# Joining two state scans into one instruction in a fused selective-scan and feed-forward kernel

## The reference

```python
dt  = softplus(dt_r @ dt_proj_w.T + dt_bias)          # per channel and token
A   = -exp(A_log)                                     # per channel and state
dA  = exp(dt_t[..., None] * A)                        # decay
dBx = dt_t[..., None] * B_t[:, None, :] * x_t[..., None]   # inflow
h   = dA * h + dBx                                    # state
y   = einsum('bdn,bn->bd', h, C_t)                    # sum over the states
```

## Time and profile before

| | us |
|---|---|
| median of three runs | 4897.68 |
| profiled execution, whole | 4888.99 |
| its span, first to last instruction | 4887.2 |
| dt*x of one step to the next, ordinary step | 34.42 to 34.43 |
| the same across the seventh step of a chunk | 37.04 |
| across the eighth | 38.95 |
| across the first of the next | 43.04 |

### The profile page before, as it was taken

One profiled execution on the slowest core, in us unless ns is written; L12 is line 12 of the kernel. 1 busy time (PEld: TensorE's weight loads), 2 busy tenths in 40 slices (PEclk: granted clock), 3 DMA queues, 4 the chain that ended last, 5 costly groups with the idle time before them and its releaser, 6 DMA issues.

```text
span 4887.2 us, 73028 instructions
## 1 busy us (share of the span) xinstructions
PE 4584.8 (94%) x22816; PEld 3921.1 (80%) x22816; DVE 4506.2 (92%) x7793; ACT 3554.9 (73%) x8720; POOL 3922.7 (80%) x2218
## 2 busy tenths in 40 slices
PE   7788989999999999999999999999999999999889
PEld 6667778888887888888888788888888888887668
DVE  3999989999999999999999999999999999999991
ACT  3677777777777777777777777777777777777660
POOL 0888878888787888888888887888888888888880
PEclk9889999999999999999999999999999999999999
DMA  7324243343434334343353434334343343434222
GB/s 252 118 76 157 101 150 131 114 175 123 167 134 148 139 130 167 123 167 122 123 181 117 171 127 159 131 122 171 133 168 120 131 162 123 162 120 146 87 107 93
DMA packets 157828, 677.85 MB, mean 139 GB/s; under 512 B 18816, under 2 KB 27648, under 8 KB 108288
## 3 DMA queue, kind: packets, MB, share of 16 engines
q1 hardware_dynamic: 139008, 639.62, 36.9%
q10 hardware_dynamic: 18432, 33.56, 1.8%
HBM read 618.06 MB, written 55.05 MB: 138 GB/s over the span
## 4 chain that ended last, share of the span: by engine, by line
POOL 61%; issue 20%; PE 8%; DVE 4%; DMA 3%; ACT 2%; POOLq 1%; SPq 1%; DVEq 0%; ACTq 0%
POOL dbx L444 38%; POOL half L452 19%; POOL dtx L467 3%; DVE hb L1289 2%; DMA bb<-bc_scratch 2%; PE g L695 2%; PE gx L525 2%; PE ys L505 1%; PE hb L788 1%; DMA ybuf<-in_wf_scales 1%; DMA bc_scratch<-ssmT 1%; DVE hc L1236 1%; ACT hb L997 1%; PE ys L545 1%; POOL x L460 1%
## 5 line engine op out<-in xcount | busy, mean ns | idle before, releaser
L1289 DVE TENSOR_TENSOR_SCAN hb<-hb,hstate,dbx 128x256 f32<-128x256 f32 x4096 | 2838.8, 738 | 140.0 <-ACT hb L997 86.8
L444 POOL TENSOR_TENSOR dbx<-dtx,bb 128x1024 f32<-128x1024 f32 x1024 | 2416.4, 2360 | 438.4 <-DVE hb L1289 347.3
L997 ACT ACTIVATE hb<-dt,a_neg 128x256 f32<-128x256 f32 x4096 | 1789.4, 468 | 66.6
L452 POOL TENSOR_TENSOR half<-hc 128x512 f32<-128x512 f32 x1024 | 1302.0, 1271 | 301.3 <-DVE hc L1236 270.5
L1236 DVE TENSOR_TENSOR hc<-hb,cb 128x512 f32<-128x512 f32 x2048 | 1373.0, 670 | 0.0
L505 PE MATMUL ys<-half,ident 128*128 128x256 f32 x4096 | 1109.3, 395 | 165.6 <-POOL half L452 165.5
L505 PEld LDWEIGHTS ys<-half,ident 128*128 128x128 f32 x4096 | 766.2, 195 | 327.4 <-POOL half L452 223.8
L545 PE MATMUL ys<-xnT,wz 128*128 128x256 f32 x4096 | 968.1, 391 | 57.8 <-DVE ybuf L1247 57.8
L695 PE MATMUL g<-ybuf,wo 128*128 128x256 f32 x3840 | 948.6, 391 | 0.7 <-issue 0.7
L545 PEld LDWEIGHTS ys<-xnT,wz 128*128 128x128 f32 x4096 | 784.9, 196 | 193.9 <-DVE ybuf L1247 89.2
L525 PE MATMUL gx<-xnT,wx 128*128 128x256 f32 x3968 | 900.5, 380 | 2.0 <-issue 1.6
(11 more groups left out here) (104 smaller groups left out, 2482.2 us busy)
## 6 DMA issues: line engine op xcount, KB each, us to landing
wz<-in_win SPq DMA_DIRECT2D x128, 1024.0 KB, 4.8
wx<-in_win SPq DMA_DIRECT2D x124, 1024.0 KB, 4.8
wo<-in_wout SPq DMA_DIRECT2D x123, 1024.0 KB, 5.0
wf<-wf_scratch SPq DMA_DIRECT2D x113, 512.0 KB, 3.3
xc_scratch<-xcn ACTq DMA_DIRECT2D x128, 256.0 KB, 2.0
xcs<-xc_scratch SPq DMA_DIRECT2D x128, 256.0 KB, 5.0
bb<-bc_scratch SPq DMA_DIRECT2D x64, 512.0 KB, 7.3
cb<-bc_scratch SPq DMA_DIRECT2D x64, 512.0 KB, 6.4
```

The lines of the kernel that those rows point to most:

```text
L444: nc.gpsimd.tensor_tensor(dbx[:, k % 2, :].rearrange("p (n t) -> p n t", n=NQ), dtx[:, a * T:(a + 1) * T].unsqueeze(1).to_broadcast([P, NQ ...
L452: nc.gpsimd.tensor_tensor(half[:, k % 4, :], hc[:, k % 2, 0:HALF], hc[:, k % 2, HALF:GW], ALU.add).then_inc(halves, 1)
L997: ins = nc.scalar.activation(h[:, m * T:(m + 1) * T], dt[:, j % 2, a * T:(a + 1) * T], ACT.Exp, scale=a_neg[:, ds((2 * j + a) * N + 2 * v ...
L1289: ins = nc.vector.tensor_tensor_scan(h[:, m * T:(m + 1) * T], h[:, m * T:(m + 1) * T], dbx[:, k % 2, (2 * w + m) * T:(2 * w + m + 1) * T], ...
```

## The change

The scan of a unit becomes one instruction of 128x512 over both states, with a constant 0.0 as its initial value. For that, column 0 of every decay is made zero, and column 0 of every inflow is made the whole state at the chunk's first token: the carried state times the first decay, plus the first inflow.

- Column 0 of `dt` holds a constant 1e19, so that exp(dt*A) is 0 there (`A` is held at or below -1e-16). Softplus writes columns 1 to 255 of both tiles in one instruction and the two first columns into `dt0`. The bias of dt moves into the matmul as a 65th row, so `ssmT` and `ssn` get one row more.
- ScalarE computes `decay0` (two instructions of 128x16) between softplus and the skip term.
- GpSimd gets `inflow_of` (dt*x of the first columns, then of the others), moved ahead of inflow 7 of the step before; `carry_of` (first inflows from a broadcast `b0`, and decay0*hstate); and `replace_first`, which writes column 0 of the B rows `bb`: once per tile of a pair, but for the first tile of a chunk once per group.
- For groups 1 and 5 of a step GpSimd adds the two remaining 256-column parts too, and TensorE sums them with one matmul in place of two.
- SyncE stores and loads the sixteen first values of B per chunk.

The core of the diff:

```diff
+FAR, LEAST_A = 1e19, 1e-16
@@ SyncE
             def bc_rows(chunk):
                 sp.wait_ge(ss_evac, after(chunk + 1))
-                sp.dma_start(bc_dram[chunk], ssmT[R:E, :]).then_inc(bc_st, 16)
-                sp.wait_ge(bc_st, landed(chunk + 1))
+                sp.dma_start(bc_dram[chunk], ssmT[BC:EO, :]).then_inc(bc_st, 16)
+                sp.dma_start(b0_dram[chunk].unsqueeze(1), ssmT[BC:BC + N, 0:1]).then_inc(bc_st, 16)
+                sp.wait_ge(bc_st, landed(2 * (chunk + 1)))
+                sp.dma_start(b0[:, chunk % 2, :], b0_dram[chunk].partition_broadcast(P)).then_inc(b0_in, 16)
@@ GpSimd
+            nc.gpsimd.memset(dt[:], FAR).then_inc(zeroed, 1)
+            def replace_first(a, lo, hi):
+                nc.gpsimd.tensor_tensor(bb[:, lo:hi, 0], carried[:, a * N + lo:a * N + hi], inflow0[:, a, lo:hi],
+                                        ALU.add).then_inc(b_first, 1)
             def group_of_b(S, k, chunk):
                 a, q = divmod(k, NQ)
+                fresh = S % PAIRS == 0 and a == 0
+                pool.wait_ge(bb_in[q], landed(chunk + 1))
+                if k == 0:
+                    pool.wait_ge(inflow, after(S + 1))
+                    pool.wait_ge(carry, after(S + 1))
+                if fresh:
+                    replace_first(a, NQ * q, NQ * (q + 1))
+                    pool.wait_ge(b_first, after(first_inflows(S) + q + 1))
+                elif q == 0:
+                    pool.wait_ge(dbxs, after(8 * S + k))
+                    replace_first(a, 0, N)
+                    pool.wait_ge(b_first, after(first_inflows(S) + (3 if S % PAIRS == 0 else 0) + a + 1))
                 pool.wait_ge(scans, after(UNITS * S + 2 * k - 2))
...
             def group_sum(S, k):
...
+                both = nc.gpsimd.tensor_tensor(half[:, k % 4, :], hc[:, k % 2, 0:HALF], hc[:, k % 2, HALF:GW],
+                                               ALU.add)
+                if k % NQ != 1:
+                    both.then_inc(halves, 1)
+                    return
+                both.then_inc(pair_sums, 1)
+                pool.wait_ge(pair_sums, after(2 * S + k // NQ + 1))
+                nc.gpsimd.tensor_tensor(half[:, k % 4, 0:T], half[:, k % 4, 0:T], half[:, k % 4, T:HALF],
                                         ALU.add).then_inc(halves, 1)
...
+            def inflow_of(S):
+                pool.wait_ge(sp_act, after(S + 1))
+                pool.wait_ge(xc_in[S % 2], landed(S // 2 + 1))
+                nc.gpsimd.tensor_tensor(dtx0[:], dt0[:, S % 2, :], xcs[:, S % 2, 0:2 * T:T], ALU.mult
+                                        ).then_inc(dtx0_ready, 1)
...
+            def carry_of(S):
...
+                nc.gpsimd.tensor_tensor(inflow0[:], dtx0[:].unsqueeze(2).to_broadcast([P, 2, N]),
+                                        b0[:, chunk % 2, :].unsqueeze(1).to_broadcast([P, 2, N]), ALU.mult
+                                        ).then_inc(inflow, 1)
+                pool.wait_ge(first_decays, after(S + 1))
+                pool.wait_ge(kept, after(UNITS * (S - PAIRS + 1)))
+                nc.gpsimd.tensor_tensor(carried[:], decay0[:], hstate[:, 2 * j * N:2 * (j + 1) * N], ALU.mult
+                                        ).then_inc(carry, 1)
@@ GpSimd, one step
                     for k in range(1, 8):
+                        if k == 7 and zz:
+                            inflow_of(S + 1)
                         group_of_b(S, k, c)
...
                     if zz:
-                        next_step(S + 1)
+                        carry_of(S + 1)
+                        group_of_b(S + 1, 0, (S + 1) // PAIRS)
                     group_sum(S, 6)
@@ TensorE, group_sum
-                for i in range(2):
+                for i in range(1 if q == 1 else 2):
@@ ScalarE, pair_softplus
-                for a in range(2):
-                    ins = nc.scalar.activation(dt[:, q % 2, a * T:(a + 1) * T], ys[1][:, a * T:(a + 1) * T],
-                                               ACT.Softplus, bias=dtb[:, ds(2 * jq + a, 1)])
-                ins.then_inc(sp_act, 1)
+                nc.scalar.activation(dt0[:, q % 2, :], ys[1][:, 0:2 * T:T], ACT.Softplus)
+                nc.scalar.activation(dt[:, q % 2, :, 1:T], ys[1][:].rearrange("p (a t) -> p a t", a=2)[:, :, 1:T],
+                                     ACT.Softplus).then_inc(sp_act, 1)
                 nc.scalar.preload_act_table_set(BASE)
+                act.wait_ge(sp_act, after(q + 1))
+                act.wait_ge(carry, after(q))
+                for a in range(2):
+                    ins = nc.scalar.activation(decay0[:, a * N:(a + 1) * N], a_neg[:, (2 * jq + a) * N:(2 * jq + a + 1) * N],
+                                               ACT.Exp, scale=dt0[:, q % 2, a:a + 1])
+                ins.then_inc(first_decays, 1)
@@ VectorE, scan
-                        for m in range(2):
-                            ins = nc.vector.tensor_tensor_scan(
-                                h[:, m * T:(m + 1) * T], h[:, m * T:(m + 1) * T],
-                                dbx[:, k % 2, (2 * w + m) * T:(2 * w + m + 1) * T],
-                                hstate[:, ds((2 * j + a) * N + 2 * v + m, 1)], ALU.mult, ALU.add)
-                        ins.then_inc(scans, 1)
+                        nc.vector.tensor_tensor_scan(h[:], h[:], dbx[:, k % 2, w * UW:(w + 1) * UW], 0.0, ALU.mult,
+                                                     ALU.add).then_inc(scans, 1)
```

More of the change, by code:

```diff
@@ L22 @@
 E = R + 2 * N
+EO = E + 1
+BC = R + 1
 NQ = 4
@@ L83, in build_program @@
 def build_program(nc, x, win, wout, wf_codes, wf_scales, ffn_bias, xproj, dtw_in, convw_in, convb_in,
-                  dtb_in, alog_in, dparam_in, lnw_in, out):
+                  alog_in, dparam_in, lnw_in, out):
     ctx = ExitStack()
@@ L144, in build_program @@
         ssm = sb("ssm", [P, TT, E])
-        ssn = sb("ssn", [P, TT, E])
+        ssn = sb("ssn", [P, TT, EO])
         sq = sb("sq", [P, TT, E])
         ssq = sb("ssq", [P, 6])
-        ssmT = sb("ssmT", [E, T])
-        dt = sb("dt", [P, 2, 2 * T])
-        dtx = sb("dtx", [P, 2 * T])
+        ssmT = sb("ssmT", [EO, T])
+        dt = sb("dt", [P, 2, 2, T])
+        dtx = sb("dtx", [P, 2, 2, T])
+        dt0 = sb("dt0", [P, 2, 2])
+        dtx0 = sb("dtx0", [P, 2])
+        b0 = sb("b0", [P, 2, N])
+        decay0 = sb("decay0", [P, 2 * N])
+        carried = sb("carried", [P, 2 * N])
+        inflow0 = sb("inflow0", [P, 2, N])
         gate = sb("gate", [P, 2, 2 * T])
@@ L837, in _ @@
             nc.scalar.preload_act_table_set(BASE)
-            act.wait_ge(zeroed, after(4))
+            act.wait_ge(zeroed, after(8))
             def norm_start(n, mv, rstd, nmr, stats, ln, r, nm):
@@ L929, in chunk_ss_out @@
                 act.wait_ge(dt_mm, after(chunk * PAIRS))
-                act.wait_ge(bc_st, landed(chunk))
-                nc.scalar.activation(ssmT[:], ys[1][0:E, 0:T], ACT.Identity, scale=lnw[:]).then_inc(ss_evac, 1)
+                act.wait_ge(bc_st, landed(2 * chunk))
+                nc.scalar.activation(ssmT[:], ys[1][0:EO, 0:T], ACT.Identity, scale=lnw[:]).then_inc(ss_evac, 1)
             def pair_softplus(q):
```

64 lines of the change are left out of this document (40 added, 24 removed).

## The result

The changed kernel took 4834.81 us (median of 4 runs, 4832.99 to 4835.69), the kernel before 4896.67 (4 runs beside them): ratio 0.9873, 95% interval 0.9861 to 0.9886. The forecast was 4905, range 4865 to 4985. Of the 70 us between forecast and result, 61 are the change itself (+7 forecast, -54 measured between the two profiled executions); the other 9 are the 8.7 that the forecast added because the median before lay above the profiled execution. After the change the two agree, 4834.81 and 4834.86.

The account below looks back on a forecast made before the run. A ring through four engines bounds the 34.42 us step, VectorE's 34.30 just below. Terms 16 - 24 + 7.5 - 2.4 + 1.3 + 8.4 = +7 on 4889.0 give 4896, plus 8.7 for the median: 4905 us, range 4865 to 4985.

Parts of the forecast that it names:

- one ring: Closed loop of waits in an ordinary step, through TensorE, ScalarE, VectorE and GpSimd back to TensorE's sum 7: 34.42 us.
- sign of being wrong: Ordinary steps under 34.2 us would mean the ring was not the bound, or a kept leg had slack.
- the four legs: Stretches of the ring by engine: TensorE 18.78, ScalarE 3.63, VectorE 2.16, GpSimd 9.85 us, together 34.42.
- The scan: One VectorE scan for two: -0.15 us per unit, its work down 2.4 us, the ring -0.15.
- TensorE's term: Sum 1, between sum 7 and the dt projection, loses one of two matmuls: -0.43 us on the ring.
- GpSimd's term: Sum 5 to inflow 0: second sum and small instructions replace dt*x, +0.55 us on the ring, between +0.2 and +1.1.
- The line through the two large sizes: GpSimd cost from 512 and 1024 columns: 2.13 ns a column and 0.18 us fixed, used to price its added instructions.
- the rival with the small price: GpSimd's small instructions cost 0.10 us each, the scan saves 0.25: ring -0.22, 4873 us; chance 0.20.
- chunk ends: At 15 chunk ends, an added store, load and replacements against earlier VectorE and ScalarE: +0.5 us each, +7.5 in all.
- Seventh steps: In 14 seventh steps of a chunk, VectorE's spare time takes up most statistics: 35.35 us, -1.7 each, -24 in all.
- The clock rival: TensorE's wait ahead of sum 7 reaches 1.7 us or more and its clock drops: 4968 to 5031 us; chance 0.25.
- Last chunk: There the ring passes sums 1 and 2 on GpSimd: +1.2 us in each of 7 steps, +8.4 in all.

Follow-up runs that it names:

- second sum once: Changed kernel with GpSimd's second sum for group 1 only, group 5 again by two matmuls on TensorE: 4780.35 us, ratio 0.9770.
- carry ahead of sum 5: Changed kernel with GpSimd's first inflows, carried states and column replacement moved ahead of sum 5, except at chunk ends: 4776.37 us, ratio 0.9761.
- decays later: Changed kernel with the two small first-token decays behind unit 12's decays on ScalarE instead of ahead: 4799.22 us, ratio 0.9804.
- 64 rows: Changed kernel with the dt projection over 64 rows again, the bias left out: 4854.43 us, ratio 0.9922.
- the dear scans: Changed kernel with two 128x256 scans per unit again, each with its carried-state column as initial value: 4895.72 us, ratio 1.000.

## Why the prediction was wrong, step by step

**That one ring sets the step: right.** VectorE's work fell by 2.4 us a step and the step by 0.22. At 34.21 us it lies on the edge of what the prediction had named as its sign of being wrong, under 34.2; but the four legs add up to it, and no leg had slack. Four edits on single legs (second sum once, carry ahead of sum 5, decays later, 64 rows) moved them by -0.81, -0.99, -0.39 and +0.20 us, and the step by -0.80, -0.98, -0.40 and +0.20.

**The scan: right in size** (1.13 to the product's start against the 1.15 that I took; 1.222 for the record, forecast 1.15 to 1.25), with the reason incomplete: most of it is the initial column, which the prediction has only in a bracket, not the instruction saved. Nor is the initial column tied to joining: two scans with a constant would have given all but 7 us of the change.

**TensorE's term: wrong, -0.43 for -0.62.** This is the step that failed first. "Its four records (two matmuls) take 0.86 ...; one matmul goes: -0.43" is right: sum 1 takes 0.43 now. But the dt projection, a landmark at the end of that same leg, was changed too, from 64 to 65 rows, and I priced that edit at nothing without saying so. It was worth 0.20, for weight loads that no longer start late where the row count changes.

**GpSimd's term: +0.55 for +0.35.** The second sum (0.69) and the first inflows (0.20, forecast 0.22) were right. The line through the two large sizes overstated what surrounds them: sum 5 to the second sum took 1.34, not 1.44, the replacement 0.31 to the next start, not 0.39. The 0.05 for more waits in a row came, in the carried states (0.48 against 0.26 and 0.17). The forecast here was between its bounds of +0.2 and +1.1, but the rival with the small price (ring -0.22) had named, by other terms, the ring that was measured. Its time, 4873, was still 38 above the result, mainly for the chunk ends below and the 8.7 of the median. The two terms, of TensorE and of GpSimd, make 27 of the 61 us. (The forecast's own range was also added up wrongly: half of the distances to -0.53 and +1.17 over 70 steps are 27 and 33 us, so 4878 to 4938 and not 4882 to 4935. The time lies far below either.)

**Seventh steps: right** (-2.0, forecast -1.7), and the experiment with the carried column as initial value shows that the scans alone did it: it gave 37.04 again.

**Chunk ends: wrong, -2.1 each for +0.5.** This is the largest miss in us, 32 of the 61 between the forecast's +7 and the measured -54. What is new there comes to +1.15 in the prediction's own numbers; I took +0.5, so VectorE's relief got 0.65 by guess ("but VectorE and ScalarE arrive earlier"), though VectorE falls behind at a chunk's end for the same reason as in the seventh step. With the dear scans, eighth and first step took 82.3; with the cheap ones 80.3, and 79.9 as two instructions. In the changed kernel the store of B and C leaves 30.1 us after the eighth step's inflow 0, with the dear scans 32.1, and before the change 32.8. The path from that store to inflow 0 of the next chunk was mis-sized too: it grew from 9.0 to 11.6 us, where I had counted 0.8 for a store and a load more and 0.39 for the replacement. VectorE's third scan behind the layer norm's statistics, the first to need that inflow, had no wait before (first line); after the change it waits for it (second fence):

```profile
2158.82 1.38 DVE L1289 TENSOR_TENSOR_SCAN hb<-hb,hstate,dbx 128x256 f32<-128x256 f32 x2
```

```profile
2136.10 0.67 DVE L1321 TENSOR_TENSOR hc<-hb,cb 128x512 f32<-128x512 f32 x1
2138.99 1.23 DVE L1373 TENSOR_TENSOR_SCAN hb<-hb,dbx 128x512 f32<-128x512 f32 x1 [2.22 <-POOL dbx L490]
```

Counted from inflow 0 to inflow 0, the eighth step went from 41.8 to 41.7 and the first from 40.6 to 38.6. With the dear scans these are 43.6 and 38.7, so the first step's gain isn't the scans', the eighth's is; what shortened the first wasn't tried.

**The clock rival: wrong for ordinary steps, right for chunk 1.** The wait ahead of sum 7 grew to 1.49 us, the forecast's 1.5, and sum 7 stayed at 1.13; the granted clock is 1.00 in each of the 60 ordinary steps. The 1.7 at which I had let it decide isn't a limit: the wait of 1.77 ahead of 2032.57 left sum 7 at 1.13, and in chunk 1 a wait of 2.37 left sum 6 at 1.13, while sum 7 behind it took 2.07 after 2.40. So the length of one wait alone doesn't say whether the clock falls. The Trainium skill (TensorE: Matmul & The Clock Gate, "HAM oscillation") has loops whose waits drop the clock in each turn; the ordinary steps here don't, chunk 1 with its waits of 2.4 and more did, and filling them brought the clock back. Chunk 1 cost the change 5.4 us that the forecast hadn't.

**Last chunk: +2.2 for +8.4.** It may be that the short waits on VectorE there gave back more than the 0.7 that I had taken. No run was made on this, and the cause stays open.
